# Skip tests in a masked cross-attention loop: testing a batch's chunks of keys from the last to the first

## What is computed

```python
_lenS2 = 2048 - jax.random.randint(..., (8,), 0, max(1, 2048 // 4) + 1, jnp.int32)
_validS2 = jnp.arange(2048)[None, :] < _lenS2[:, None]
mask_BxS2_bk0 = jnp.logical_not(jnp.broadcast_to(_validS2[:, :], (8, 2048)))
...
sim = jnp.einsum('bihd,bjhd->bhij', q, k) * scale          # context: 8 x 2048 x 384
sim = jnp.where(mask[:, None, None, :], sim, max_neg)
attn = jax.nn.softmax(sim, axis=-1)
x = x + xattn(layernorm(x), ctx_768, mask_BxS2_bk0, ...)
x = x + attn(layernorm(x), ...)
x = x + ffn(layernorm(x), ...)
```

## Time and profile before

| | |
|---|---|
| median of three runs | 836.67 us |
| the profiled execution, its own time | 834.46 us |
| its span, first to last instruction | 832.5 us |
| mean granted TensorE clock | 0.926 |
| PE busy | 697.4 us (84%) |
| DVE busy | 440.3 us (53%) |
| ACT busy | 380.0 us (46%) |
| chain that ended last | PE 64%, issue 12%, DVE 8%, ACT 6%, DMA 4% |

### The profile page before, as it was taken

The page is one execution under the profiler, slowest core; times in us unless marked ns, Lnnn a source line. Parts: engine busy times, 40 slices in busy tenths (PEclk is TensorE's granted clock), DMA queues, the critical chain, the costliest instruction groups (busy, mean ns, idle before and its releaser), DMA issues.

```text
span 832.5 us, 15880 instructions
## 1 busy us (share of the span) xinstructions
PE 697.4 (84%) x4310; PEld 551.9 (66%) x4338; DVE 440.3 (53%) x964; ACT 380.0 (46%) x888; POOL 75.5 (9%) x120
## 2 busy tenths in 40 slices
PE   3978579889696969699598999999997499989994
PEld 2767468778585858587386777777776388635452
DVE  6644335534544445446477366665564124699960
ACT  3233324434342444344233466666554235368884
POOL 2480000100101010101100000000000000112211
PEclk9999789979898889799699899999996799999998
DMA  8010000000000000032488224444435912000111
GB/s 291 0 44 0 20 20 20 20 0 20 20 20 20 20 0 20 20 94 115 159 308 289 93 80 144 141 145 138 136 122 173 156 72 79 0 1 14 25 25 38
DMA packets 40133, 64.67 MB, mean 78 GB/s; under 512 B 4138, under 2 KB 20522, under 8 KB 40114
## 3 DMA queue, kind: packets, MB, share of 16 engines
q1 hardware_dynamic: 40114, 64.45, 24.4%
HBM read 53.95 MB, written 10.49 MB: 77 GB/s over the span
## 4 chain that ended last, share of the span: by engine, by line
PE 64%; issue 12%; DVE 8%; ACT 6%; DMA 4%; DVEq 3%; SPq 1%; POOL 1%; ACTq 0%; POOLq 0%
PE bank L545 35%; PE bank L680 6%; PE bank L889 5%; PE bank L806 4%; PE bank L668 3%; PE bank L897 3%; ACT p L1094 3%; DMA x_all<-x_mid_dram 2%; PE bank L653 2%; PE bank L788 2%; PE bank L797 1%; DMA wq_raw<-in_L_xattn_W_q_dram 1%; DVE oT_lo L1276 1%; PE bank L784 1%; DVE amax L1552 1%
## 5 line engine op out<-in xcount | busy, mean ns | idle before, releaser
L979 ACT ACTIVATE probs<-probs,negm 128x256 f32<-128x256 f32 x104 | 52.1, 501 | 105.3 <-DVE negm L1401 105.3
L1401 DVE CUSTOM_DVE_ANT_0 probs<-bank,bias,negm_old 128x256 f32<-128x256 f32 x104 | 46.0, 480 | 60.6 <-PE bank L653 58.4
L1094 ACT ACTIVATE p<-bank,nmax 128x128 f32<-128x128 f32 x128 | 45.0, 378 | 44.4 <-DVE nmax L1554 44.4
L453 POOL TENSOR_TENSOR rstd<-var_eps,neg_half 128x1 f32 (+1 forms) x16 | 10.4, 650 | 592.9 <-DVE var_eps L1623 329.4
L889 PE MATMUL bank<-w_T,xqT 128*128 128x512 bf16 x248 | 57.3, 379 | 4.9 <-ACT xqT L1163 2.0
L653 PE MATMUL bank<-kT_hi,qT_hi 64*128 64x256 f32 x104 | 22.8, 436 | 44.7 <-issue 44.4
L680 PEld LDWEIGHTS bank<-v_sb,pT 128*128 128x128 f32 x416 | 52.3, 191 | 5.5
L680 PE MATMUL bank<-v_sb,pT 128*128 128x64 f32 x416 | 54.7, 274 | 0.0
L972 ACT COPY v_sb<-bank 128x512 f32<-128x512 f32 x28 | 15.1, 590 | 76.5 <-PE bank L680 73.5
L1276 DVE TENSOR_TENSOR kT_lo<-bank,kT_hi 128x512 fp32r<-128x512 f32 x28 | 19.4, 692 | 57.8 <-ACT kT_hi L968 57.8
L653 PEld LDWEIGHTS bank<-kT_hi,qT_hi 64*128 64x128 f32 x104 | 11.1, 210 | 54.0 <-issue 47.0
(11 more groups left out here) (213 smaller groups left out, 1664.6 us busy)
## 6 DMA issues: line engine op xcount, KB each, us to landing
tern_dram<-tern SPq DMA_DIRECT2D x8, 768.0 KB, 3.6
tstage<-tern_dram SPq DMA_DIRECT2D x8, 768.0 KB, 5.6
cx<-in_ctx_dram SPq DMA_DIRECT2D x14, 384.0 KB, 3.0
absw<-in_L_ffn_w_gate_dram SPq DMA_DIRECT2D x8, 512.0 KB, 3.8
absw<-in_L_ffn_w_up_dram SPq DMA_DIRECT2D x8, 512.0 KB, 4.8
absw<-in_L_ffn_w_down_dram SPq DMA_DIRECT2D x8, 512.0 KB, 6.1
tern_raw<-in_L_ffn_w_gate_dram SPq DMA_DIRECT2D x8, 512.0 KB, 4.6
tern_raw<-in_L_ffn_w_up_dram SPq DMA_DIRECT2D x8, 512.0 KB, 5.8
```

The costliest lines, as they stand in the source:

```text
L979: fn(probs[:, h, :], probs[:, h, :], ACT.Exp, bias=negm[:, h:h + 1], scale=-1.0, accum_out=csum[:, h:h + 1]).then_inc(p_done, 1)
L1094: last = fn(p2[:, j, g * P:(g + 1) * P], bank[2 + j][:, g * P:(g + 1) * P], ACT.Exp, bias=nmax2[:, j, g:g + 1], scale=SCALE, accum_out=sum ...
L1401: nc.vector.tensor_tensor_reduce(probs[:, h, :], bank[3 + h % 2][:, 0:CHUNK], bias[:], -SCALE, negm_old[:, h:h + 1], ALU.add, ALU.min, neg ...
```

## The change

The powers of two in `weight4` are filled in the opposite order, so that bit c of a batch's number now stands for chunk 7 - c, and SP, the only engine that turns c into an address, computes the address of chunk 7 - c. The four loops now visit the chunks from the last to the first: in this input the turns of the live chunks come first, and the turns of the dead ones after them. Within a batch with two live chunks these two swap places. Nothing else is touched.

```diff
-                            load_chunk((b * NC + c * UNROLL + u) * CHUNK)
+                            load_chunk((b * NC + (NC - 1) - c) * CHUNK)
...
-                nc.gpsimd.memset(weight4[:, c:c + 1], float(1 << c)).then_inc(consts, 1)
+                nc.gpsimd.memset(weight4[:, c:c + 1], float(1 << (NC - 1 - c))).then_inc(consts, 1)
```

## The result

The changed kernel takes 845.26 us (median of 8 runs, 841.02 to 846.55); the kernel before, run beside it on the same chip, 836.43 (8 runs). The ratio is 1.0096, 95% interval 1.0074 to 1.0117: **slower by about 1%**, and outside the predicted range. The profiled execution took 845.12 us with a span of 843.4, so the spans differ by 843.4 - 832.5 = 10.9 us. The mean granted clock is 0.926 in both.

The account below looks back on a forecast made before the run. Dead-chunk tests were taken to hold up each batch's first scores, DVE's setting the time after batch 2. Terms -3.0 - 1.0 - 0.35 + 0.3 + 4.7 + 1.8 + 1.2 - 2.6 = +1.05 gave 837.7 us, range 832.5 to 843.

Parts of the forecast that it names:

- The exchange of tests, 0: Between batches: six tests behind the path exchanged for six ahead, net 0; X is DVE's last add of a batch.
- The head, -3.0: Start of the loop: PE's tests ahead of batch 0's scores go, first maximum at 62.9 instead of 65.90, -3.0 us.
- Chunk 0, -1.0: First chunk of the loop: the gap ahead of its scores goes, so its loss to the low clock returns, -1.0 us.
- The boundaries, +2.65: Last add to next first maximum at seven boundaries, from the terms for tests and low clock: +2.65 us in all.
- the tail, +5.0: Last add of batch 7 to the self-attention's first matmul: +5.0 us, DVE's six tests ahead of `on_c` giving +4.7.
- the term for `project_output`: Its 12 matmuls between batches may run at low clock: +0.3 six times from batch 2 on, +1.2 after batch 1.
- Of the 4.4 us lost in later chunks I take back -2.6: Chunks after chunk 0: PE's work between two gaps lets the clock rise earlier, -2.6 us (between -4.4 and +5).
- 6.5 us cost 1.2 and 3.5 cost nothing: First chunks after a boundary: 6.5 us at low clock lengthen the chunk by 1.2 us, 3.5 us by nothing.
- The slower rival: Low clock moves into the path at `project_output`, over half its 12 matmuls at 1.2 GHz: +13.2, 850 us, chance 0.12.
- its three signs: Add-to-maximum mean changes over 1 us; clock 0.50 through `project_output`; or DVE's tests run while it waits for the add.
- Cold jumps: Batch ends: each first jump back over the chunk's body costs DVE 0.4 us, eight give +3.2; 841 us, chance 0.08.
- Theory A: Stated after the result: the exchange of tests is neutral; the clock makes the loss, in `project_output` and in the chunks.

Follow-up runs that it names:

- e2: The kernel before, with three small matmuls that nobody reads added on PE in each dead turn; 838.6 us, ratio 1.0007.
- e1: The changed kernel, with three small matmuls that nobody reads added on PE in each dead turn; 841.34 us, ratio 1.0044 to the kernel before.
- e8: The changed kernel, with the loop ending when no live chunk is left in the batch; 812.34 us, ratio 0.9699 to the kernel before.
- e6: The kernel before, with four chunks tested at once and single tests only in a group with a live chunk; 823.45 us, ratio 0.9858.
- e10: The kernel before (old order), with the loop ending when no live chunk is left, which leaves out no test here; 833.02 us, ratio 0.9969.
- e5: The changed kernel, with unread matmuls on PE in dead turns, ahead of turn_output and behind turn_norm; 838.87 us, ratio 1.0023 to the kernel before.
- e11: The changed kernel, with an added wait and jump in PE's dead turns but no extra matmuls; 867.17 us, ratio 1.0344 to the kernel before.

## Why the prediction was wrong

- **The exchange of tests, 0: right.** `on_c` at X+7.4, 0.7 us from DVE's live test to the maximum. Between batches 4 and 5 the boundary fell by 0.4 (forecast -0.8), between 5 and 6 it grew by 0.8 (forecast +0.8).
- **The head, -3.0: -2.3.** The gap went, but the scores started at 62.84, 0.7 later than forecast from the values' last matmul: the clock was 0.50 from 53.4 to 56.8, ahead of the loop. That spell was not in the terms, and isn't the change's: of either order some traces have such a spell (e2 from 51.2 to 58.0) and some have none (the kernel before, e1).
- **Chunk 0, -1.0: right.** 18.62 to 17.58, and the low spell inside it (67.2 to 70.6) is gone.
- **The boundaries, +2.65: +5.0; the tail, +5.0: +5.75.** From batch 2 on the term for `project_output` held: five boundaries grew by 1.95, forecast 1.5, although it took 4.5 to 5.5 us instead of 3.0, because 1.3 us of that is slack. After batch 1, where there is no slack, the 2.5 us of the low clock arrived whole (the boundary went from 10.07 to 12.94, with 0.3 for the tests): 1.2 was taken for it, and 2.5 was its upper bound. Between 0 and 1 the +0.2 instead of -0.35 fits the low clock over 84.1 to 97.8, but no run tells it apart.
- **The step that failed: "Of the 4.4 us lost in later chunks I take back -2.6". Measured: +3.8** (the 12 chunks behind chunk 0 went from 215.39 to 219.17). This step alone makes 6.4 of the 9.8 us between forecast and result. The reason given, that work between the gaps lets the clock rise earlier, came true; what it missed is that the clock falls again inside the chunk. Its bounds (-4.4 to +5) held the value, but the range of the sum didn't carry them through.
- **"6.5 us cost 1.2 and 3.5 cost nothing": wrong as read.** It took the length of a low spell for its price. It is the place. Chunks of several runs, numbered 0 to 12 in the order of the run, with the low spell counted from the chunk's first maximum:

| low clock, us from first maximum | run, chunk | lost over 17.58 |
|---|---|---|
| -4.71 to 2.12 | before, 2 | 0.0 |
| -3.29 to 3.54 | before, 6 | 0.5 |
| -2.27 to 4.55 | e8, 1 | 1.0 |
| -5.12 to 5.12 | before, 4 | 1.2 |
| 3.10 to 6.51 | after, 4 | 1.5 |
| 0.91 to 7.73 | e8, 2 | 2.4 |

Low clock within the first 2.3 us or so costs nothing, and each us behind that costs some 0.43 (worked out from these chunks: 1.5 / 3.4, and 2.4 / 5.4). This holds in all kept traces: of their 182 chunks, 180 lost what it gives to within 0.15 us. The two others are chunk 0 of e6 and of e10, which lost 0.7 at a clock of 1.00; ACT's first exponential came 0.7 us later there. That PE isn't the one waited for in a chunk's first us would explain it; this wasn't tried by itself. A spell of 6.8 us costs 0 in one chunk and 2.4 in another. The changed kernel's second spell lies in the part that costs: chunks 4, 8, 9 and 11 lose 1.4 to 1.5 us each by it, and chunk 2 0.9. Chunk 1 loses 1.5 by the end of a long first spell (84.1 to 97.8).

- **The slower rival, 850 us with a chance of 0.12,** came nearer than the forecast (845.26 measured). It had the right place and decided as it said it would: more than half of the 12 matmuls ran at 1.2 GHz, behind each of batches 1 to 7. The prediction named this as a sign of being wrong, and of its three signs it is the one that came; the distance from add to maximum changed by 0.7 us on the mean. Its price was 12.5 us without the other terms; it got too much for the transposes and the slack-covered boundaries, and nothing for the chunks. The argument against it, that `project_output` is dense work that lifts the clock by itself, fell: the clock rose in its last third or behind it (at 268.4 for the one from 263.95 to 269.0). The rule of the Trainium skill cited there ("TensorE: Matmul & The Clock Gate", Part 1: The HAM clock gate), that an idle stretch brings the half clock back, agrees with the windows above for the first fall. The second followed no idle stretch, but one in which PE was busy for 2.92 of 5.10 us.
- **Cold jumps, 0.08:** didn't happen. DVE's dead tests behind a live chunk took 0.78 us each, and `on_c` started at X+7.4 as worked out from them, so the jump back over the chunk's body left no 0.4 us.

Theory A stands for the larger part: filling the gaps gave back 0.73% of the 0.96% (e5). The table of parts says the same, by a sum and not by a run. Its 11.2 us hold 2.7 in the chunks, 2.6 behind batch 1, 1.95 in the other five and 1.05 in the tail where `project_output` is slow, together 8.3 of the clock; 1.65 of the tests (-3.0 - 0.35 + 0.3 + 4.7), as forecast; and 1.25 in the head and between batches 0 and 1. By that estimate the order itself costs some 0.2%: the tests that it adds at the end (4.7) are more than those that it takes from the head (3.0). What stays open is the rest. e5's interval still lies just above 1, and its dead turns are longer than the changed kernel's; how much of the rest is longer tests and how much the order itself wasn't told apart, since e11 was no clean control.

## What to carry to other kernels

Moving idle time is not free even where the path stays as long: ask what TensorE does right behind the new gap, and price a low clock by the place where it ends, not by its length. A reordering that moves tests wins nothing by itself, but it may allow leaving them out: ending the loop early won 3.0%, and a few matmuls that nobody reads in the remaining gaps 0.8% more. And before costing a cut at its own duration, look at what the removed work was keeping apart.

## What the runs showed of the hardware

- A spell at 1.2 GHz can follow a stretch in which PE is only thinly used. Before the fall at 275.3 PE was busy for 2.92 of 5.10 us; in e5, with three matmuls more behind `turn_norm`, the clock stayed at 1.00 at that boundary, though it still fell in two other chunks (at 123.8 and 349.1).
- DVE's normalisation of 128x512 (`xn_c`) and POOL's residual delay each other, and 0.1 us decides which is delayed. Of the 112 normalisations in the 14 traces, 66 took 0.55 us: POOL started at least 0.103 us behind them, or was long done. The other 46 took 1.44 to 1.65: POOL started between 0.105 us ahead and 0.096 us behind. Why is not shown here.
- A skipped turn costs by how it is written: on PE 0.85 us in the counted loop, and in e10's loop that ends on a zero register 0.60 us, on DVE 0.43 instead of 0.78:

```profile
L265 PEldq ALU_OP  x8: 36/36/36, 87.2 to 91.4; - x8
L265 DVEq ALU_OP  x8: 45/45/45, 88.4 to 91.4; - x8
```

Eight tests, seven steps: (91.4 - 87.2) / 7 and (91.4 - 88.4) / 7. A body with nothing but a wait made the turn 0.2 us dearer than one with three matmuls besides (1.3 against 1.1).
